# Rotary attention: a quarter of the denominators summed by the vector engine, the other exponentials written back into their score bank

## The reference

```python
attn_num = jnp.exp(jnp.einsum('bhqd,bhkd->bhqk', q_rot, k_rot) / scale)
attn_den = jnp.exp(jnp.einsum('bhqd,bhkd->bhqk', q, k) / scale)
attn_den = jnp.sum(attn_den, axis=-1, keepdims=True)
attn = attn_num / attn_den
causal = jnp.tril(jnp.ones((c, c), jnp.float32))[None, None]
attn = jnp.where(causal == 0, 0.0, attn)
y = jnp.einsum('bhqk,bhkd->bhqd', attn, v)
```

## Time and profile before

| | us |
|---|---|
| median of 3 runs | 1890.01 (1889.61 to 1891.53) |
| profiled execution | 1893.23 |
| its span | 1891.5 |
| PE / DVE / ACT / POOL busy | 1643.9 / 1192.6 / 1442.4 / 314.4 |
| first exponential of the rotary attention | 884.20 |
| last accumulator read of it | 1710.7 |

### The profile page before, as it was taken

How to read it: one execution, slowest core, us unless ns; L and a number is a source line. 1 busy time by engine, 2 the same in 40 slices (tenths; PEclk the granted TensorE clock), 3 DMA queues, 4 the chain that set the end, 5 groups by cost and what they waited for, 6 DMA issues and landing times. The chain is left out here.

```text
span 1891.5 us, 33776 instructions
## 1 busy us (share of the span) xinstructions
PE 1643.9 (87%) x12964; PEld 630.1 (33%) x12964; DVE 1192.6 (63%) x2130; ACT 1442.4 (76%) x2508; POOL 314.4 (17%) x420
## 2 busy tenths in 40 slices
PE   5799999999999999864888888989889888883995
PEld 3222222222222222251333333433343333222674
DVE  7999989999999999886454536354545423223220
ACT  4478777777777777724999999999989999992221
POOL 4500010010011010032000100010001032312466
PEclk9899999999999999977999999999999999996997
DMA  5311111111111110004111211123111222231433
GB/s 169 99 38 38 38 44 38 38 44 38 38 38 44 39 40 19 12 21 151 45 43 55 85 58 51 53 68 98 51 47 63 86 82 93 96 118 59 124 57 30
DMA packets 70960, 115.86 MB, mean 61 GB/s; under 512 B 10041, under 2 KB 55973, under 8 KB 66192
## 3 DMA queue, kind: packets, MB, share of 16 engines
q1 hardware_dynamic: 59536, 92.88, 15.5%
q0 software_dynamic: 11264, 20.83, 4.0%
HBM read 71.49 MB, written 42.14 MB: 60 GB/s over the span
## 5 line engine op out<-in xcount | busy, mean ns | idle before, releaser
L786 ACT ACTIVATE rows_and_probs<-psS 128x512 f32<-128x512 f32 x1010 | 549.1, 596 | 166.7 <-PE psS L684 165.9
L808 DVE TENSOR_REDUCE max_of_halves<-psM 128x2 f32<-128x1024 f32 x512 | 623.6, 1224 | 54.6 <-PE psM L647 20.3
L1647 ACT ACTIVATE exps<-cpsS 128x1024 bf16<-128x1024 f32 x512 | 546.3, 1109 | 25.4 <-PE cpsS L1389 24.8
L1389 PE MATMUL cpsS<-rotary_stack 128*128 128x512 bf16 x1024 | 301.8, 384 | 72.4 <-ACT exps L1647 30.7
L704 PE MATMUL psO<-rows_and_probs,plain_v 128*9 128x256 f32 x4096 | 317.7, 382 | 5.3 <-ACT rows_and_probs L786 0.6
L1657 ACT ACTIVATE cprobs<-cpsS 128x1024 f32<-128x1024 f32 x256 | 281.7, 1100 | 21.6 <-PE cpsO L1422 18.9
L1369 PE MATMUL cpsS<-rotary_stack 128*128 128x512 bf16 (+3 forms) x768 | 193.6, 329 | 53.6 <-ACT exps L1647 36.5
L647 PE MATMUL psM<-plain_top 64*128 64x512 bf16 x1024 | 205.8, 384 | 20.9 <-DVE max_of_halves L808 20.5
L684 PE MATMUL psS<-plain_top 64*128 64x512 bf16 x1010 | 208.4, 388 | 0.0
L684 PE MATMUL psS<-plain_rest 64*128 64x512 bf16 x1010 | 202.6, 378 | 0.0
L1422 PE MATMUL cpsO<-cprobs,rotary_v 128*9 128x512 f32 (+3 forms) x1536 | 153.7, 488 | 0.8 <-DVE rotary_sums L1981 0.8
(11 more groups left out here) (301 smaller groups left out, 1758.2 us busy)
## 6 DMA issues: line engine op xcount, KB each, us to landing
rotary_stack<-q_parts SPq DMA_DIRECT2D x48, 192.0 KB
rotary_stack<-k_parts SPq DMA_DIRECT2D x48, 192.0 KB
rotary_stack<-q_rot_parts SPq DMA_DIRECT2D x48, 192.0 KB
rotary_stack<-k_rot_parts SPq DMA_DIRECT2D x48, 192.0 KB
tokens_taken<-parts_and_sums POOLq DMA_DIRECT2D x32, 259.0 KB, 4.1
plain_top<-q_parts SPq DMA_DIRECT2D x64, 96.0 KB
plain_top<-k_parts SPq DMA_DIRECT2D x64, 96.0 KB
e_x<-tokens_taken SPq DMA_DIRECT2D x8, 518.0 KB, 9.8
```

Of the source, the lines that this page charges most:

```text
L786: act.activation(pr[n % SLOTS_P][:, h, :], score_bank(u), ACT.Exp, scale=SCALE).then_inc(s_e, 1)
L808: dve.tensor_reduce(mh[g % 2][cq][:, :, hh, t, kh:kh + 1].rearrange("p e o -> p (e o)"), psM[n % 2][:, :, :], AX.X, ALU.max).then_inc(s_r, 1)
L1389: ins = pe.matmul(to[:, kh, :], q[:, x, y_ * P:(y_ + 1) * P], k[:, x, kh * CH:(kh + 1) * CH], start=True, stop=True)
L1647: act.activation(ex[d % EX][:, :, :], psS[n % 3][:, :, :], ACT.Exp, scale=SCALE, accum_out=den[:, at:at + 1]).then_inc(s_e, 1)
```

## The change

Of the 32 `den` units of a group, those with `d % 4 == 3` (8 of them, `ADDED`) are handled in a new way in all groups but the last. Their exponential goes to one float32 tile `exps` of 128 x 1024 without an accumulator. DVE adds the two halves of that tile and sums the result into the column of `den` (`add_exps`). DVE's instruction for this is the pair that is printed below as `ISA`. ACT waits before the next such exponential until the last one has been added (`s_ds`), and DVE waits for the exponential (`s_e`). All other `den` exponentials keep the accumulator, but write back into the bank pair that they read, and the wait for the ring of two `exps` tiles is gone. In DVE's program the add of a unit stands at the start of the step of the next unit, ahead of that step's tasks. The merge of a group waits for the group's adds.

```diff
@@ late_phase @@
-    EX, STORES, HTS = 2, 3, TC
+    STORES, HTS = 3, TC
+    ADDED = [d for d in range(NDEN) if d % 4 == 3]
...
-        ex = [sb(f"exps{i}", [P, 2, CH], BF16) for i in range(EX)]
+        ex = sb("exps", [P, 2, CH])
+        s_ds = sem("exps_added")
@@ scalar engine, exps(g, u) @@
-                    if g * NDEN + d >= EX:
-
-                        act.wait_ge(s_e, made[(d - EX) % NDEN] + (g if d >= EX else g - 1) * U + 1)
+                    if d in ADDED and g < G - 1:
+                        if g or d != ADDED[0]:
+
+                            act.wait_ge(s_ds, g * len(ADDED) + ADDED.index(d))
+                        act.wait_ge(s_s, n + 1)
+                        act.activation(ex[:, :, :], psS[n % 3][:, :, :], ACT.Exp, scale=SCALE).then_inc(s_e, 1)
+                        return
                     act.wait_ge(s_s, n + 1)
                     at = g * NDEN + d
-                    act.activation(ex[d % EX][:, :, :], psS[n % 3][:, :, :], ACT.Exp, scale=SCALE,
+
+                    act.activation(psS[n % 3][:, :, :], psS[n % 3][:, :, :], ACT.Exp, scale=SCALE,
                                    accum_out=den[:, at:at + 1]).then_inc(s_e, 1)
@@ vector engine @@
+                if g < G - 1:
+
+                    dve.wait_ge(s_ds, (g + 1) * len(ADDED))
...
+            def add_exps(g, d, u):
+
+                dve.wait_ge(s_e, g * U + u + 1)
+                at = g * NDEN + d
+                dve.tensor_tensor_reduce(ex[:, 0, :], ex[:, 0, :], ex[:, 1, :], 1.0, 0.0, ALU.add, ALU.add,
+                                         den[:, at:at + 1]).then_inc(s_ds, 1)
...
             for g in range(G):
                 for u in range(U):
+                    n, (kind, x, y_) = g * U + u - 1, seq[u - 1]
+                    if 0 <= n < (G - 1) * U and kind == "den" and y_ * HG + x in ADDED:
+                        add_exps(n // U, y_ * HG + x, n % U)
```

## The result

The changed kernel is slower: 1904.69 us, the median of 4 runs (1901.76 to 1905.47), against 1890.77 us (4 runs, 1889.61 to 1891.63). The ratio is 1.0068 with a 95% interval of 1.0056 to 1.008. The forecast was 1878.0 us, 12 us faster, with a range up to 1897.

The account below looks back on a forecast made before the run. The prediction took ACT's pitches plus 35 us of gaps in the rotary attention stage as the bound. Terms -11.0 - 5.9 + 3.7 + 1.2 = -12.0 us took the 1890.0 us median to 1878.0, range 1863 to 1897.

Parts of the forecast that it names:

- What bounds the stage: Rotary attention stage: its end is set by the sum of ACT's start-to-start pitches plus 35 us of gaps.
- The reads that go: ACT: 120 accumulator reads dropped, each giving back 0.092 us of pitch, -11.0 us.
- The destination: ACT: the other 392 exponentials write to PSUM instead of SBUF, gaining 0.015 us each, -5.9 us.
- The bound upwards (+43): Worst case for 392 PSUM writes: the next instruction cannot start under the 0.11 us tail, +43 us.
- rival E: ACT: writing into the bank being read stops the next instruction starting under the tail; +43 us, 1927 us; chance 0.11.
- turning point: Cost of each PSUM write from which rival E was said to decide: 0.015 us.
- The adds, 0.76 us: DVE: 120 adds of 0.69 us plus 0.07 for the accumulator read; by itself costing nothing.
- Rival D: DVE's add streams at half rate and the PSUM destination gives nothing; slower, 1897 us; chance 0.14.
- The first chain: ACT's next added exponential waits for the previous add on the single tile; 4 of 120 late, +3.7 us.
- The second chain: DVE waits for exponentials, delaying copies that empty `cpsB`; 17 of 183 fills pushed, 6 reaching ACT, +1.2 us.
- Its example: Group 5's denominator 19: its add makes the following DVE chain 2.7 us late and PE's scores some 0.6 us late.

Follow-up runs that it names:

- e2: The change, but the other 392 exponentials go to two bfloat16 tiles in SBUF instead of their bank: 1898.8 us, ratio 1.0032.
- e6: The change with two bfloat16 tiles for added exponentials, each add 2 units later, the other exponentials to SBUF: 1881.5 us, ratio 0.9949.
- e1: The change without DVE adds: all 512 denominators keep their accumulator and write back into their score bank: 1896.3 us, ratio 1.0025.
- e4: Kernel before with four forms of the denominators' exponential side by side, half the sums left out; only pitches read, 0.942 us into PSUM without accumulator.
- e5: As e2, but the added exponentials alternate between two bfloat16 tiles, adds at the change's own place: 1894.3 us, ratio 1.0019.
- e9: As e6, with four more denominators of each group added by DVE, twelve instead of eight: 1888.3 us, ratio 0.9974.

## Why the prediction was wrong

**What bounds the stage.** Right. Pitches and idle time add up to the stage by construction; what bears the step out is that the stage's change carries the kernel's in every row of the table: +14.1 of 13 to 14 us in the change, +6.6 of 6.1 in e2, -8.8 of 9.6 in e6, and within 2 us elsewhere.

**The reads that go, -11.0.** Right: 1.003 less 0.908 is 0.095, over 120 that is 11.4 us, and e2 has it in its pitches (-9.4, with those that stand before a wait).

**The destination, -5.9.** This step failed, and in sign. I took the numerator's exponential as nearest and a quarter of 0.054 us as a gain. Measured is a loss of 0.027 to 0.030 us in each pitch, 11 us over 392 where ACT does not wait, of which 0.0036 to 0.0041 of the time (7 to 8 us) reaches the end beside the adds, and 4.7 us in e1 without them. The bound upwards (+43) did hold it, and rival E had the sign. E's mechanism was not it: e4 has the same pitch for the same bank and for the other one. The prediction gave E 0.11 and called its turning point 0.015 us a write; the measured cost is twice that. It also named a shift of this pitch by more than 0.03 us as a sign of being wrong, and the shift is about that size.

The Trainium skill's rule that ScalarE is closer to PSUM and PSUM the lower-latency destination ("ScalarE: Activation LUTs", Step-by-step: what each stage is for) does not carry over to the pitch here: the record is shorter (1056 against 1109 ns), the pitch longer. By that rule taken to its end the sum was 15 us lower than mine, and the chip went the other way.

**The adds, 0.76 us.** Right: 0.693 and 0.083 us. Rival D falls, since the add does not stream at half rate.
The Trainium skill's rule that a scalar-tensor-tensor form with two non-bfloat16 sources in SBUF halves its throughput ("Vector Engine (DVE) Microarchitecture Reference", 7. Points that are easy to get wrong) is not borne out for this instruction: two float32 sources take 0.69 us in the changed kernel, two bfloat16 ones 0.68 in e6.

**The first chain, +3.7.** Right as a wait: 3.6 us, at group 5 2.16 for 2.3. What I left out is that PE stands still behind it and its clock falls (940.1 and 1155.1), though ACT shows no further long idle time there. And e5 takes this wait away and gains too little for its interval to tell, so it was not where the loss lay.

**The second chain, +1.2.** This step failed by its size, ten times. The idle time grew by 16.1 us, 3.6 of them the first chain's; that leaves 12.5. The step counted "17 of 183 fills" of `cpsB`, that is only the copies that empty that bank, and let 6 of them reach ACT with 1.2 us. The number of places was not far off: PE's matmuls into `cpsB` wait for DVE 12 times in the changed kernel (3 before), the weight loads in front of them 28 times (13 before), most of these under 1 us. What was missed is the few long ones. The largest losses came from the copy of `cpsO` (3.73 us of ACT's idle time in one place) and from rows that DVE makes and PE transposes (2.46). It also held PE's durations fixed, and the clock at half made them longer just where PE was late. The clock is the smaller part of it. e2 and e5 differ by 2.0 us of idle time at one such place, and there are three in the changed kernel, so I estimate some 4 to 6 of the 12.5 us for the clock and the rest for lateness; no run holds the clock and moves the lateness alone over the whole stage. That lateness costs without the clock e9 shows: 9.8 us more than e6 and no fall. The prediction had called this chain its least certain count, but gave it 10.2 us only for an add at half rate; the add ran at full rate and the chain cost that much all the same. (Its example also takes 1.02 us for an exponential that the earlier trace rows have with 1.09, which changes nothing.)

**Together.** Of the 26 us between -12.0 and +14.1, 15 are in the pitches and 11 in the idle time. With the write to PSUM and nearly all of the waits taken out (e6) the reads that go give 0.9949, -9.6 us, of -11.0 forecast. That rival D's time (1897) lies nearest to the measured 1904.7 is luck: its cause, the add at half rate, is not there.

## What to carry to other kernels

An add that waits for another engine stalls everything behind it in its program. Choose its place by the work that stands behind it: here two units later gave 13 us, more than the change was to bring, although DVE still waited 68 us for its exponentials, and four units later gave less, because ACT then waited for a tile. Try more than one place. When such a wait is followed, follow everything the delayed engine produces (other banks' copies, computed operands), not only the obvious buffer, and count the slow clock after PE's idle time. A destination whose price no row shows can have either sign even if its record is shorter: measure the pitch of one such instruction first.

## What the runs showed of the hardware

- An exponential of 128 x 1024 from PSUM back to PSUM has a pitch of 0.942 us against 0.904 to SBUF (e4, where both records are 1.03 us long), and it makes no difference whether 512 elements go back to the bank that they come from or to the other one (0.603 us both). With the accumulator read the pitches are 1.030 and 0.997 us (after, e4).
- An accumulator read on ACT costs 0.09 us of pitch (1.003 less 0.908 before, 1.030 less 0.942 into PSUM), whatever its record says (227 ns on average after, 294 before).
- DVE sums two streams of 512 float32 with an accumulator in 0.69 us, the time of a plain add of 512 (692 ns), plus 0.08 for the read.
- At 1390.7 us in the changed kernel, behind a stretch of 3.4 us in which PE was busy for 0.62, its granted clock fell to 0.50 and stayed there up to 1394.1; the same eight matmuls took 1.90 us instead of 1.04. The fall made 2.0 us more of ACT's idle time out of one wait of 2.75 us (e5 against e2).
